# Loads begun by SP instead of ScalarE, two activation tables asked for ahead, one GpSimd split put behind a normalisation, and scaled identities made ahead of a residual addition

## The reference, cut to what matters

```python
x = x + attn(layernorm(x))                 # causal, projections with bias
x = x + xattn(layernorm(x), ctx)           # cross attention over 77 context tokens
x = x + ffn(layernorm(x))

def ffn(x):                                # 704 hidden
    xq   = fake_quant(x, clip_x)           # sigmoid(clip) * max|x| / 127, one scale for all of x
    gate = xq @ row_quant(w_gate).T
    up   = xq @ row_quant(w_up).T
    h    = fake_quant(silu(gate) * up, clip_down)
    return h @ row_quant(w_down).T         # row_quant: one scale per row, max|w| / 127
```

## Time and profile before

| | |
|---|---|
| three runs | 989.15, 990.71, 991.78 us (median 990.71) |
| the profiled execution | 986.81 us |
| its span in the trace | 985.1 us |
| busy: TensorE, weight loads | 899.3 us (91%), 440.0 us (45%) |
| busy: VectorE, ScalarE, GpSimd | 710.8 (72%), 601.1 (61%), 313.9 us (32%) |
| cross attention of the last sample | from about 797 to 876 us |
| feed-forward | from 886.3 us |

### The profile page before, as it was taken

The page is one execution under the profiler, slowest core; times in us unless marked ns, Lnnn a source line. Parts: engine busy times, 40 slices in busy tenths (PEclk is TensorE's granted clock), DMA queues, the critical chain, the costliest instruction groups (busy, mean ns, idle before and its releaser), DMA issues. The chain is left out here.

```text
span 985.1 us, 17246 instructions
## 1 busy us (share of the span) xinstructions
PE 899.3 (91%) x6003; PEld 440.0 (45%) x6018; DVE 710.8 (72%) x1467; ACT 601.1 (61%) x1118; POOL 313.9 (32%) x348
## 2 busy tenths in 40 slices
PE   4788999999999989999999999999999998988976
PEld 2433443455544534464446343554444454543344
DVE  3889866768766783777777928777674568778977
ACT  2335577746576577447675775456788624637974
POOL 1351135330431218413431165313512122203723
PEclk9979999999999999999999999999999999999999
DMA  5340111335222142101220313202210243115009
GB/s 164 108 124 17 56 58 53 76 60 82 82 77 73 43 146 76 55 17 56 92 88 17 126 45 99 63 31 82 87 49 2 86 150 100 37 38 171 1 9 184
DMA packets 83568, 73.42 MB, mean 75 GB/s; under 512 B 19244, under 2 KB 79788, under 8 KB 83484
## 3 DMA queue, kind: packets, MB, share of 16 engines
q1 hardware_dynamic: 75772, 66.17, 22.2%
q0 software_dynamic: 4256, 3.21, 2.6%
q10 hardware_dynamic: 3456, 2.94, 1.0%
HBM read 19.81 MB, written 13.13 MB: 33 GB/s over the span
## 5 line engine op out<-in xcount | busy, mean ns | idle before, releaser
L767 ACT ACTIVATE probs<-psum 128x512 f32<-128x512 f32 (+1 forms) x608 | 314.6, 577 | 179.5 <-PE psum L962 176.6
L1136 DVE CUSTOM_DVE_ANT_0 junk<-psum,mask 128x640 bf16<-128x640 f32 (+3 forms) x256 | 253.4, 1022 | 59.4 <-PE psum L926 57.2
L684 POOL TENSOR_SCALAR_AFFINE_SELECT probs<-probs 128x512 f32<-128x512 f32 x128 | 81.6, 640 | 391.5 <-ACT probs L767 391.2
L962 PE MATMUL psum<-q_stack,k_stack 98*128 98x512 bf16 (+3 forms) x768 | 188.0, 331 | 6.7 <-DMA q_stack<-max_rows 2.6
L987 PE MATMUL psum<-probs,v_sb 128*17 128x512 f32 (+3 forms) x1536 | 158.9, 492 | 3.8 <-POOL probs L684 3.4
L1132 DVE TENSOR_REDUCE rowmax<-psum 128x4 f32<-128x512 f32 (+2 forms) x96 | 97.3, 1045 | 62.9 <-PE psum L920 62.5
L926 PE MATMUL psum<-k_stack,q_stack 96*128 96x512 bf16 (+3 forms) x512 | 128.7, 344 | 5.8 <-DVE rowmax L1136 4.5
L962 PEld LDWEIGHTS psum<-q_stack,k_stack 98*128 98x128 bf16 x768 | 62.7, 98 | 136.6 <-ACT probs L767 80.9
L886 PE MATMUL psum<-xnT,wT 128*128 128x512 f32 x192 | 90.8, 604 | 0.6 <-ACT xnT L732 0.5
L811 PE MATMUL psum<-wT,xnT 128*128 128x256 f32 x384 | 87.6, 385 | 0.4 <-ACT xnT L732 0.3
L811 PEld LDWEIGHTS psum<-wT,xnT 128*128 128x128 f32 x384 | 73.3, 193 | 12.6 <-ACT xnT L732 1.2
(11 more groups left out here) (180 smaller groups left out, 1242.7 us busy)
## 6 DMA issues: line engine op xcount, KB each, us to landing
q_stack<-q_parts SPq DMA_DIRECT2D x192, 64.0 KB, 2.6
k_stack<-k_parts SPq DMA_DIRECT2D x192, 64.0 KB, 2.6
xq_stack<-xq_parts SPq DMA_DIRECT2D x168, 64.0 KB, 2.6
xn<-in_x SPq DMA_DIRECT2D x8, 512.0 KB, 5.0
res<-in_x SPq DMA_DIRECT2D x4, 1024.0 KB, 6.8
out<-res SPq DMA_DIRECT2D x8, 512.0 KB, 2.9
normT_hbm<-xnT SPq DMA_DIRECT2D x6, 512.0 KB, 3.9
xf<-normT_hbm SPq DMA_DIRECT2D x6, 512.0 KB, 3.7
```

The costliest lines, as they stand in the source:

```text
L684: nc.gpsimd.affine_select(out=tile, in_=tile, compare_op=ALU.is_ge, fill=0.0, base=0, pattern=[[0, GH], [1, P]], channel_multiplier=-1).th ...
L767: nc.scalar.activation(probs[n % 2][:, heads * k:heads * k + heads, 0:cols], bank_a(s)[:, 0:heads * cols].rearrange("p (h n) -> p h n", h= ...
L962: last = nc.tensor.matmul(bank[:, cols * n:cols * n + cols], k_stack[:, slot, h, P * j:P * j + P], q_stack[:, slot, half, h, q0 - HALF * h ...
L1136: nc.vector.tensor_tensor_reduce(out=junk[D_STEPS.place(s) % 2][:, 0:keys], in0=bank_d(s)[:, 0:keys], in1=m.mask[:, T - keys:T], scale=1.0 ...
```

## The change

Five edits are made.

1. ScalarE issues only the two first weights and one bias tile. The six other weights, the context, the biases and the clips are issued by SP, behind the rows of ones and a wait for x's second half.
2. ScalarE runs an Exp over two constants, into a tile that nobody reads, ahead of its first wait. In the feed-forward it runs a Silu over the two clips, likewise, ahead of its wait for `x_scaled`.
3. GpSimd's split of `("q", 1, 3, 1, 0)` waits also for the last `apply` piece of the last sample's second normalisation.
4. The two scaled identities become a step of their own, `wdiag`, ahead of `("o", 1, 3, 1)`. `wrow` stays where it was, but takes a bank of ring A, and ScalarE copies the row out.
5. The 24 fillers at `wrow` go, and 20 are put ahead of `("xT", 2, 3, 0, 1)`.

But for `wdiag`, all steps stand in `ORDER` as they did.

```diff
-A_KINDS = ("s2", "xT", "yT", "q", "k", "mT", "xs2", "xy", "kx", "wT", "wdT")
-D_KINDS = ("s1", "xs1", "o", "v", "yN", "xyN", "vx", "wrow")
+A_KINDS = ("s2", "xT", "yT", "q", "k", "mT", "xs2", "xy", "kx", "wT", "wdT", "wrow")
+D_KINDS = ("s1", "xs1", "o", "v", "yN", "xyN", "vx")
...
-        [("wT", 1, c) for c in range(CC)] + tiles[2 * FT:] + [("wdT", n) for n in range(2)] + [("wrow",)]
+        [("wT", 1, c) for c in range(CC)] + tiles[2 * FT:] + [("wdiag",)] + [("wdT", n) for n in range(2)] + [("wrow",)]
...
-    "ddcddccdxxdyxccwwddddxxddxwdxdddddwddxdyyxwwxxxyyyyyywwwyyy")
+    "ddcddccdxxdyxccwwddddxxddxwdxdddddwddxdyyxwwxxxwyyyyyywwwyyy")
...
-    if kind == "wrow":
-        return 24
...
-                ("q", 1, last, 0, 0): 3, ("xT", 1, last, 0, 1): 24, ("q", 1, last, 0, 1): 2, ("xT", 2, last, 0, 0): 2}.get(s, 0)
+                ("q", 1, last, 0, 0): 3, ("xT", 1, last, 0, 1): 24, ("q", 1, last, 0, 1): 2, ("xT", 2, last, 0, 0): 2, ("xT", 2, last, 0, 1): 20}.get(s, 0)
...
         def _(sp):
+            def load_rest():
+
+                sp.wait_ge(x_in[1], 16)
+                for n in range(2, 8):
+                    sp.dma_start(m.wT[:, n, :, :], w["attnT"][n].rearrange("(a p) o -> p a o", p=P)).then_inc(rest_in, 16)
+                sp.dma_start(ctxT, w["ctxT"].rearrange("(a p) n -> p a n", p=P)).then_inc(rest_in, 16)
+                for n in range(4):
+                    sp.dma_start(m.bias_f[n][:, :], w["bias_f"][n].partition_broadcast(P)).then_inc(small_in, 16)
+                for n in range(2):
+                    sp.dma_start(m.clips[:, n:n + 1], w[("clip_x", "clip_d")[n]].partition_broadcast(P)).then_inc(small_in, 16)
...
                                      ones_row[:, 0:S].unsqueeze(1).to_broadcast([SHIFT_ROWS, H * B, S])).then_inc(ones_in, 16)
+                        load_rest()
...
                     pool.wait_ge(*a_emptied(s))
+                    if s[1:] == (1, B - 1, 1, 0):
+
+                        pool.wait_ge(normed, NORMS.upto(("ln", 1, B - 1, "apply", 3)))
...
             def load_weights():
...
                 for n in range(2):
-                    act.dma_start(m.clips[:, n:n + 1], w[("clip_x", "clip_d")[n]].partition_broadcast(P)).then_inc(small_in, 16)
+                    act.dma_start(m.wT[:, n, :, :], w["attnT"][n].rearrange("(a p) o -> p a o", p=P)).then_inc(qk_in, 16)
+                act.dma_start(m.bias_t[:], w["bias_t"]).then_inc(bias_in, 16)
+
+                act.wait_ge(ones_done, 3)
+                nc.scalar.activation(unread[:], m.ones[:, 0:2], ACT.Exp)
                 act.wait_ge(bias_in, 16)
...
+                if s[0] == "wrow":
+                    nc.scalar.activation(m.dscale_f[:], bank_a(s)[:, 0:C], ACT.Copy).then_inc(a_free, 1)
...
                     pe.wait_ge(diag_done, CC)
-                    bank = next_pair(s)
+                    bank = next_bank(s)
...
-                    last.then_inc(d_full, 1)
+                    last.then_inc(a_full, 1)
...
-                if s[0] == "wrow":
+                if s[0] == "wdiag":
                     for o in range(CC):
                         nc.vector.tensor_scalar(diag[:, o, :], m.ident[:], dscale[:, o:o + 1], None,
                                                 ALU.mult).then_inc(diag_done, 1)
-                    dve.wait_ge(d_full, D_STEPS.upto(s))
-                    nc.vector.tensor_copy(m.dscale_f[:], bank_d(s)[:, 0:C]).then_inc(d_free, 1)
...
             nc.scalar.activation(small[:, BOTH_EXPC], m.clips[:], ACT.Exp, scale=-1.0).then_inc(clip_exp, 1)
+
+            nc.scalar.activation(small[:, UNREAD], m.clips[:], ACT.Silu)
             act.wait_ge(x_scaled, 1)
```

More of the change, by code:

```diff
@@ L433, in run_layers @@
         bmax = sb("bmax", [P, 1])
+        unread = sb("unread", [P, 2])
         ones_row = sb("ones_row", [SHIFT_ROWS, P], BF16)
@@ L689, in load_weights @@
             def load_weights():
-                for n in range(8):
-                    if n == 2:
-                        act.wait_ge(x_in[1], 16)
-                    act.dma_start(m.wT[:, n, :, :], w["attnT"][n].rearrange("(a p) o -> p a o", p=P)).then_inc(
-                        qk_in if n < 2 else rest_in, 16)
-                    if n == 1:
-                        act.dma_start(m.bias_t[:], w["bias_t"]).then_inc(bias_in, 16)
-                act.dma_start(ctxT, w["ctxT"].rearrange("(a p) n -> p a n", p=P)).then_inc(rest_in, 16)
-                for n in range(4):
-                    act.dma_start(m.bias_f[n][:, :], w["bias_f"][n].partition_broadcast(P)).then_inc(small_in, 16)
                 for n in range(2):
-                    act.dma_start(m.clips[:, n:n + 1], w[("clip_x", "clip_d")[n]].partition_broadcast(P)).then_inc(small_in, 16)
+                    act.dma_start(m.wT[:, n, :, :], w["attnT"][n].rearrange("(a p) o -> p a o", p=P)).then_inc(qk_in, 16)
+                act.dma_start(m.bias_t[:], w["bias_t"]).then_inc(bias_in, 16)
+                act.wait_ge(ones_done, 3)
+                nc.scalar.activation(unread[:], m.ones[:, 0:2], ACT.Exp)
                 act.wait_ge(bias_in, 16)
@@ L1063, in _ @@
             for s in ORDER:
-                if s[0] in D_KINDS and s[0] != "wrow":
+                if s[0] in D_KINDS:
                     dve.wait_ge(d_full, D_STEPS.upto(s))
@@ L1215, in feed_forward @@
         TOP, XSC, XINV, HLOC, HSC, HINV = (slice(n, n + 1) for n in (4, 5, 6, 7, 8, 9))
-        BOTH_EXPC, BOTH_SIG = slice(0, 2), slice(2, 4)
+        BOTH_EXPC, BOTH_SIG, UNREAD = slice(0, 2), slice(2, 4), slice(12, 14)
         clip_exp = sem("clip_exp")
```

## The result

| | before | after |
|---|---|---|
| timed side by side, median of 20 runs each | 991.91 us (986.33 to 998.04) | 990.13 us (983.65 to 994.76) |
| ratio after to before | | 0.9962, 95% interval 0.9945 to 0.998 |
| timed again, 12 runs against 23 | 993.08 us | 987.95 us, ratio 0.9944 (0.992 to 0.9969) |
| the profiled execution, its span | 986.81, 985.1 us | 991.5, 989.7 us |
| mean granted clock of the profiled execution | 0.988 | 0.980 |

What follows compares the result with a forecast made beforehand. It took four places on the path to the end as bound by the instruction releasing each next stage, not by TensorE's average. Gains 0 + 1.7 + 0.75 + 0.45 = 2.9 us gave 987.8 us, range 985.3 to 991.8.

Steps and rivals of the forecast that it cites:

- A: First 20 us: loads on SP and Exp table ahead gain 0, since TensorE waits for the context's DMA anyway.
- B: Last sample's second normalisation: GpSimd's split waiting behind it brings the negated score maxima 1.7 us sooner.
- C: End of the layers: scaled identities made sooner and the row copied by ScalarE gain 0.75 us.
- D: First feed-forward tiles: loading the Silu table ahead gains 0.45 us of the 1.28 us load.
- Rivals 2 and 3: At the start: context lands 1.5 us sooner, 986.3, chance 0.08; or 1.3 us later, 989.1, chance 0.08.
- The exact meeting: At the score maxima: the negation's second half starts just ahead of GpSimd's next instruction, unhurt; maxima at 823.5, not 825.2.
- Rival 1: At the score maxima: GpSimd's third instruction gets in first, the negation's second half waits about 1.15 us; 989.0, chance 0.20.
- The slack of 0.4 us at the stacks: Last sample's scores: the tightest stack lands about 841.7, scores run at 842.1, so the 1.7 us gain passes.
- Rival 4: Handover to the feed-forward: TensorE's clock falls into the first four tiles, 5.1 us lost, 2.2 net; 992.9, chance 0.12.
- its own sign: Handover: a granted clock reading below 1 between 882 and 894 us would show the prediction wrong.
- Rival 5: Whole kernel: a stack or a collision of VectorE and GpSimd takes the gains back; 990.7, chance 0.06.
- The base: Whole kernel before: median 990.71 us of three timed runs, 2.6 us apart, from which the gain was subtracted.

Runs made afterwards that it cites:

- before again: The kernel before, unchanged, profiled a second time; that execution took 995.9 us instead of 986.81.

## Why the prediction was right, and where it wasn't

| part | predicted | traces | shown by |
|---|---|---|---|
| A, start | 0 (1.5 gained to 1.3 lost) | 0, to a few tenths | issue to landing, ten profiles |
| B, split behind the normalisation | 1.7 (0 to 2.06) | 1.80 | wait undone: 16.05 |
| C, identities and row | 0.75 (0 to 1.05) | 0.93 | undone: 10.07 and 16.91 |
| D, Silu ahead | 0.45 (0 to 1.28) | 0.49 | undone: 9.36 |
| sum | 2.9 | 3.2 | |
| fall of the clock at the handover | -5.1 with a chance of 0.12 | -1.8 to -2.0, in 4 of 9 profiles | see below |
| fall of the clock in the last projection | not in the sum | 1.7 gained: 4 of 4 profiles without edits 4 and 5, 0 of 10 with them | not shown why |

**A** held, and its reason with it: the wait for the context hides ScalarE, and with that cover moved away the two kernels differ by 3.45 us. Rivals 2 and 3 fell: no landing came 1.5 us sooner or 1.3 later. What the part left out is the moment at which TensorE reaches its full rate, which scatters more than any of this: the values' projection starts 13.15 us behind the first transposes in one profile of the kernel before and 14.03 in the other, with the change 13.30 to 14.87.

**B** held step by step. The normalising instructions take 1.38 us; the transposes stay behind the fillers; the quick split's third takes 0.69. One size was off: two small instructions meet GpSimd, not one, 0.57 instead of 0.17 us and 1.10 instead of 0.35, so 1.15 us of the 2.1 are lost again and not 0.75. The quick split therefore starts when VectorE's queue has come to it, 10.39 us behind the fillers' start, and not when its input is ready (10.24), where the working had it. The two lie so close together that 0.95 us are gained there and not 0.98: the sum came out right in part by this luck. The exact meeting also came out as read from the earlier trace rows: the negation's second half starts at 831.20, GpSimd's third instruction at 831.22, and the first isn't held. Rival 1 would have had the maxima 1.15 us later; it fell in all eight profiles that have this place as changed (14.23 to 14.24 us each). The slack of 0.4 us at the stacks was enough: counted from the fillers, the next residual addition comes at 48.25 us in the profile of the changed kernel and at 48.32 to 48.81 in six others with this place as changed and no fall of the clock in between, where the two of before have 50.18 and 50.00.

The rule of the Trainium skill (SBUF — State Buffer, "Who interferes with whom"), that whoever starts first holds the shared pair of ports for a whole instruction, agrees with the rows of the run with 14 fillers (a VectorE instruction of 0.28 us took 1.12 behind a GpSimd one that had started 0.20 us before it). It decides here in favour of the forecast and not of the rival, because VectorE was first, by 0.02 us in the trace.

**C**: the mechanism held, ScalarE's copies (ending at 891.16) are what now ends the block and VectorE's maximum (890.90) isn't. The terms mis-sized are the two identities, put at 0.5 us ahead of the addition, which cost 0.33, since the instructions there start 0.20 us apart, each before the one ahead has ended. What they bring behind the addition was forecast as 1.25 and measured as 1.26, so 0.93 are left instead of 0.75.

**D** held: 0.49 of 1.28 us. A page of the Trainium skill (ScalarE: Activation LUTs, "What ACT_TABLE_LOAD costs") gives a load 1283 ns, which the trace has, and about as much again for the engine's draining. No run here shows that second part: with the Silu ahead undone, the first Silu starts 1.30 us behind the load's start, and ScalarE had been idle for 5.73 us before.

**Rival 4** is where the prediction misjudged, in both numbers, and by its own sign it was wrong here. I held it for unlikely, since the idle stretches are hardly longer than before. In the changed kernel's order TensorE idles 1.56 us, works 1.1 and idles 1.0, where with the row in its old place it idled 1.39, worked 1.6 and idled 1.36. The fall stood there in 4 of the 9 profiles that have edits 4 and 5 with 20 fillers, and in none of the 4 without these edits. By chance alone, were the place no cause, the four would fall so 126 times in 715, 18%: it is a suspicion, not a finding. And I priced it at 5.1 us, as if the clock stayed down into four tiles. It fell only behind the transposes and came back as the first tile began, so what it took was the twelve fillers' 2.3 us, of which 1.98 arrive (1.76 to 2.01 in the four profiles). At four in nine that is 0.8 us of the 3.2 on average, which the two timed ratios can neither show nor exclude. The edits also seem to take a fall away in the feed-forward's last projection, worth 1.7 us (last part); the prediction had nothing of that. **Rival 5** fell: the gains stand in every profile.

**The base** was the weakest number. I took 1.3 us for the scatter from three runs; 20 runs of the kernel before spread over 11.7 us. Their median is 991.91, 1.2 us above the one used, which is half of the 2.3 us by which the forecast of 987.8 lies below the measured 990.13. The other half is that the medians moved by 1.8 us and not by 2.9, while the ratio (0.9962, forecast 0.9971) says 3.8. The forecast of the difference was good. That the measured time lies inside the range up to 991.8 is in part luck: with a fall in four of nine executions and such a scatter, either side was within reach.

## What to carry to other kernels

Ask of each part which instruction ends the stage, and compare traces by distances inside the stage: those repeat to 0.02 us in executions 9 us apart, unless the clock falls inside. Where each run's granted clock is on record, the span times that clock is a steadier measure than the span. Where two engines share something, each step sooner on a third engine can set off a new meeting: ten useless matmuls less cost 1.9 us here, because they brought GpSimd's next split 2.1 us forward. An engine freed early at the start is worth what the next one's order makes of it; here the order had to be changed with it, and even then half of the gain went into work at half rate.

## What the runs showed of the hardware that I had not expected

The granted clock explains most of the scatter: over the 23 runs of the kernel before, time and mean granted clock correlate with -0.87, over the 20 of the changed kernel with -0.90. In each profile it falls to 0.50, which is 1.2 GHz, in 6 to 10 places; the shorter of these falls cost 1.7 us of clock each, and all falls together come in the kernel before to 11.8 us in one profile and 20.5 in the other. The same code has a fall in one execution and none in the next. In the seven places that I read, TensorE had done much the same before: 1 to 2 us with little or no work, then 0.5 to 2.5 us of work, and then the clock fell. Not every fall has that shape: at 53.5 us in the kernel before, the last gaps had been of 0.75 and 0.31 us, and at 31.1 us in the changed one the clock fell while TensorE stood still. The windows of the kernel before show a place of the first kind, in the last projection of the feed-forward (columns as above).

```profile
952.00:953.00 1.00, 0.52 (x4) 0.21 (x4) 0.33 (x1) 1.00 (x2) 0.00 (x0) 1.00 0.00 0
953.00:954.00 1.00, 0.00 (x0) 0.00 (x0) 1.00 (x1) 1.00 (x1) 0.00 (x0) 1.00 0.00 0
954.00:955.00 1.00, 0.52 (x4) 0.39 (x5) 1.00 (x2) 1.00 (x1) 0.00 (x0) 0.83 0.00 0
955.00:956.00 1.00, 1.00 (x6) 0.71 (x5) 1.00 (x2) 1.00 (x2) 0.12 (x1) 0.50 0.08 16
```

TensorE stands still for 1.96 us, works again from 954.5, and is at half its clock while it is 100% busy. So a short gap has a price beyond itself. Elsewhere it is paid in some executions only; at this place it is not so. The fall stands there in all four profiles that have the row in its old place (before, before again, the moved key projection in the kernel before, row and fillers undone), and in none of the ten that have edits 4 and 5, though the gap is the same.

The timeline, in the kernel before:

```profile
954.48 7.39 PE L1353 MATMUL psum<-wdT,hq 128*128 128x256 bf16 x48 [1.96 <-DVE hq L1466]
```

And in the changed kernel:

```profile
961.10 5.72 PE L1363 MATMUL psum<-wdT,hq 128*128 128x256 bf16 x48 [1.96 <-DVE hq L1476]
```

The same 48 matmuls take 1.67 us less. From the first tile to the end of the execution it is 93.29 us with only the row and its fillers undone, and 91.10 to 92.32 in the nine profiles that have edits 4 and 5 and the Silu ahead. By chance alone four falls in fourteen profiles would sort themselves so once in 1001 times; but this was read off afterwards, among some ten places with falls, and no run tests why the clock holds there. As an estimate, 3.2 us from the stages, less 0.8 for the falls at the handover, and 1.7 for the ones missing here, make 4.1 us: inside both timed intervals (2.0 to 5.5, and 3.1 to 7.9).

The time of one execution of this kernel is therefore good to some 6 us either way, twice what the whole change brings; and a profile of the slower kernel can be the shorter one, as it was here.
